# First expert layer: the inner channels of the first product go to the partitions

## The reference, cut to what matters

```
for e in range(8):                                  # experts; each token has its best two
    w_e = sum(where(top_i == e, top_v, 0))
    h = gelu(xf @ fc1_w[e].T + fc1_b[e])            # 192 channels to 512 inner ones
    y = h @ fc2_w[e].T + fc2_b[e]                   # 512 to 192
    out = out + w_e[:, None] * y
shared = gelu(xf @ w1_w.T + w1_b) * (xf @ w3_w.T + w3_b) @ w2_w.T + w2_b
```

## Time and profile before

| | |
|---|---|
| median of 3 runs | 450.82 us (450.76 to 451.69) |
| the profiled execution: its own time | 451.97 us |
| its span | 450.0 us |
| PE busy | 405.9 us, 90% of the span |
| DVE, ACT, POOL busy | 58%, 41%, 29% |
| share of PE in the chain that ended last | 79% |
| layer 0's blocks, first product of block 0 to y of block 22 | 56.45 to 149.0 us |

### The profile page before, as it was taken

The page is one execution under the profiler, slowest core; times in us unless marked ns, Lnnn a source line. Parts: engine busy times, 40 slices in busy tenths (PEclk is TensorE's granted clock), DMA queues, the critical chain, the costliest instruction groups (busy, mean ns, idle before and its releaser), DMA issues.

```text
span 450.0 us, 7988 instructions
## 1 busy us (share of the span) xinstructions
PE 405.9 (90%) x2303; PEld 299.8 (67%) x2304; DVE 262.5 (58%) x673; ACT 186.5 (41%) x463; POOL 128.4 (29%) x137
## 2 busy tenths in 40 slices
PE   0999998999999899988888877999989999999995
PEld 0755365666667888866766655744667877778884
DVE  4535514222222187789898974574676767677744
ACT  1024232122222115798787863333344444444410
POOL 4301124455554100000000000002255555555530
PEclk9999999999999999999999999999999999999999
DMA  8999201111110387000000087780011111110006
GB/s 224 258 305 330 52 17 36 39 45 46 33 33 9 102 263 328 1 1 1 1 2 1 1 213 208 180 230 13 16 46 34 33 37 36 44 49 23 0 0 210
DMA packets 20888, 39.41 MB, mean 88 GB/s; under 512 B 5711, under 2 KB 14965, under 8 KB 20418
## 3 DMA queue, kind: packets, MB, share of 16 engines
q1 hardware_dynamic: 11362, 29.66, 22.9%
q0 software_dynamic: 5280, 6.85, 5.3%
q10 hardware_dynamic: 4224, 2.62, 2.1%
HBM read 36.21 MB, written 7.93 MB: 98 GB/s over the span
## 4 chain that ended last, share of the span: by engine, by line
PE 79%; ACT 6%; DMA 6%; DVE 4%; issue 3%; POOL 0%; ACTq 0%; DVEq 0%; SPq 0%; POOLq 0%
PE bank L1368 14%; PE bank L1282 12%; PE bank L1344 9%; PE bank L1349 8%; PE bank L1537 5%; PE bank L1360 4%; PE bank L1491 4%; DMA w_first<-y_rows 3%; PE bank L1553 3%; PE bank L1326 2%; PE bank L1355 2%; PE bank L1354 2%; PE bank L1268 2%; PE bank L1585 2%; ACT scratch L755 2%
## 5 line engine op out<-in xcount | busy, mean ns | idle before, releaser
L549 POOL DMA_INDIRECT rows<-xn_rows,slot_tok x56 | 59.4, 1061 | 89.1 <-DVE slot_tok L935 51.6
L557 POOL DMA_INDIRECT y_rows<-y,slot_row x54 | 56.0, 1036 | 86.5 <-DVE y L1003 46.1
L1368 PE MATMUL bank<-w_second,hid_t 128*128 x370 | 70.9, 331 | 6.5 <-issue 3.6
L1368 PEld LDWEIGHTS bank<-w_second,hid_t 128*128 128x128 f32 x370 | 58.7, 190 | 10.6 <-issue 10.5
L1349 PE MATMUL bank<-w_first,rows_t 128*128 x124 | 45.3, 488 | 0.4 <-issue 0.4
L1005 DVE TENSOR_TENSOR y<-bank,w_second 128x192 f32<-128x192 f32 x23 | 8.2, 358 | 63.6 <-PE bank L1368 63.6
L1344 PE MATMUL bank<-w_first,rows_t 96*128 (+1 forms) x92 | 43.5, 595 | 1.1 <-issue 1.0
L988 DVE COPY hid_t<-bank 128x384 f32<-128x384 f32 (+1 forms) x54 | 33.0, 612 | 19.2 <-PE bank L1360 13.8
L654 ACT ACTIVATE act_h<-bank 128x512 f32<-128x512 f32 x23 | 13.7, 597 | 69.6 <-PE bank L1344 69.6
L597 POOL COPY act_h<-o_inv 128x256 f32<-128x256 f32 x12 | 4.8, 402 | 122.7 <-DVE o_inv L1169 122.7
L659 ACT ACTIVATE act_g<-bank 128x384 f32<-128x384 f32 x31 | 15.2, 492 | 51.4 <-PE bank L1355 51.4
(11 more groups left out here) (198 smaller groups left out, 790.8 us busy)
## 6 DMA issues: line engine op xcount, KB each, us to landing
w_first<-in_gate_up SPq DMA_DIRECT2D x16, 384.0 KB, 6.5
w_second<-in_down SPq DMA_DIRECT2D x1, 4608.0 KB, 17.4
w_first<-in_fc SPq DMA_DIRECT2D x1, 3072.0 KB
w_second<-in_fc SPq DMA_DIRECT2D x1, 3072.0 KB, 28.2
w_first<-in_gate_up_rest SPq DMA_DIRECT2D x16, 192.0 KB, 7.2
rows<-xn_rows,slot_tok POOLq DMA_INDIRECT x56, 2.7
y_rows<-y,slot_row POOLq DMA_INDIRECT x54, 2.3
w_first<-in_x_t SPq DMA_DIRECT2D x2, 384.0 KB, 4.5
```

Source lines behind the costliest of these rows:

```text
L549: pool.indirect_dma_start(rows[b % 2][:, 0:ROW[L.l]], None, xn_rows[L.l], bass.IndirectOffsetOnAxis(slot_tok[:, b:b + 1].bitcast(U32), 0), ...
L557: pool.indirect_dma_start(y_rows[L.l], bass.IndirectOffsetOnAxis(slot_row[:, b:b + 1].bitcast(U32), 0), y[b % 2][:], None, bounds_check=TO ...
L1368: ins = pe.matmul(bank[:, 1, 0:C], hid_t[:, tile(ic)], w(P, ic * C, C), start=(ic == 0), stop=(ic == L.IC - 1))
```

## The change

In layer 0 the operands of the first product change places. For each of 4 pieces of 128 inner channels and each of 2 halves of the channels, the array holds a 96 (or 97) x 128 piece of the weights, and `rows_t`, 128 columns, is streamed: bank 5 gets the inner channels in partitions and the 128 rows along the free dimension, in 4 pieces. Gelu's output is what the second product holds, so the 4 transposes and the copy to `hid_t` are gone. `act_h` and `hid_t` become the two buffers of Gelu's output. The weights come from `first_w`, two buffers of 97 x 1024 in `scratch`, to which DVE copies the block's weights in two instructions (`copy_weights`), some blocks ahead; DVE does the `value_load` of row 0 and PE doesn't any more. The first product of b now waits for the copies and for Gelu of b-1 (it reads bank 5). DVE's loop body is: copies for b, result of b-2.

```diff
+        self.first_w_ready = sem(f"L{n}_first_w_ready")
...
+        hid_b = [act_h, hid_t]
+        first_w = [scratch_at(2048 + u * NCH * I0, NCH, I0) for u in range(2)]
...
+        def act_block0(act, L, b, u):
+            act.wait_ge(L.first_ps, b + 1)
+            nc.scalar.activation(hid_b[u][:], bank[:, 5, :], ACT.Gelu).then_inc(L.hid_ready, 1)
...
+            def copy_weights(L, b, u):
+                at = dve.value_load(blk_weights[0:1, 0, bass.ds(b, 1)], min_val=0, max_val=(L.E - 1) * L.sizes[0])
+                if not isinstance(b, int) or b >= 2:
+                    dve.wait_ge(L.first_ps, b - 1)
+                for k in range(NCH):
+                    w = w_first[0:CH + k, k * I0:(L.E - 1) * L.sizes[0] + (k + 1) * I0][:, bass.ds(at, I0)]
+                    v.tensor_copy(first_w[u][0:CH + k, k, :], w).then_inc(L.first_w_ready, 1)
...
             def blocks(L):
+                dve.wait_ge(s_fc1, 32)
+                dve.wait_ge(L.expert_ready, len(L.sizes))
+                copy_weights(L, 0, 0)
+                copy_weights(L, 1, 1)
                 dve.wait_ge(s_fc2b, 16)
-                dve.wait_ge(L.expert_ready, len(L.sizes))
-                hid_copy(L, 0)
+                copy_weights(L, 2, 0)
                 result(L, 0, 0, 0)
-                hid_copy(L, 1)
+                copy_weights(L, 3, 1)
                 result(L, 1, 1, 0)
                 w_low_parts()
-                with dve.Fori(0, (L.NB - 3) // 2) as i:
+                with dve.Fori(0, (L.NB - 5) // 2) as i:
                     for u in range(2):
-                        b = i * 2 + (u + 3)
-                        hid_copy(L, b - 1)
-                        result(L, b - 1, u, i + 1)
-                hid_copy(L, L.NB - 1)
-                result(L, L.NB - 1, (L.NB - 1) % 2, (L.NB - 1) // 2)
+                        b = i * 2 + (u + 4)
+                        copy_weights(L, b, u)
+                        result(L, b - 2, u, i + 1)
+                copy_weights(L, L.NB - 1, (L.NB - 1) % 2)
+                for b in (L.NB - 3, L.NB - 2, L.NB - 1):
+                    result(L, b, b % 2, b // 2)
...
             def first(L, b, w, u):
                 pe.wait_ge(L.rows_t_ready, b + 1)
                 if L.l == 0:
-                    for k in range(NCH):
-                        kr = CH + k
-                        ins = pe.matmul(bank[:, 5, :], rows_t[0:kr, k, :], w(kr, k * I0, I0),
-                                        start=(k == 0), stop=(k == NCH - 1))
+                    pe.wait_ge(L.first_w_ready, NCH * (b + 1))
+                    if not isinstance(b, int) or b > 0:
+                        pe.wait_ge(L.hid_ready, b)
+                    for ic in range(L.IC):
+                        for k in range(NCH):
+                            kr = CH + k
+                            ins = pe.matmul(bank[:, 5, tile(ic)], first_w[u][0:kr, k, tile(ic)], rows_t[0:kr, k, :],
+                                            start=(k == 0), stop=(k == NCH - 1))
                     ins.then_inc(L.first_ps, 1)
...
             def hid_transpose(L, b):
+                if L.l == 0:
+                    return
...
-                pe.wait_ge(L.hid_t_ready, b + 1)
+                hid = hid_t if L.l else hid_b[u]
+                pe.wait_ge(L.hid_t_ready if L.l else L.hid_ready, b + 1)
...
-                    w1 = weights(L, i * 2 + 3, 0)
+                    w1 = first_weights(L, i * 2 + 3)
```

More of the change, by code:

```diff
@@ L649, in act_rows @@
                            ).then_inc(L.rows_t_ready, 1)
+        def act_block0(act, L, b, u):
+            act.wait_ge(L.first_ps, b + 1)
+            nc.scalar.activation(hid_b[u][:], bank[:, 5, :], ACT.Gelu).then_inc(L.hid_ready, 1)
         def act_block(act, L, b):
             act.wait_ge(L.first_ps, b + 1)
[L653 to L659, removed]
+            if not isinstance(b, int) or b > 0:
+                act.wait_ge(L.hid_ready, b)
+            nc.scalar.activation(act_g[:], bank[:, 5, 0:I1], ACT.Silu).then_inc(L.gate_act, 1)
         def rest_of(start):
@@ L694, in act_blocks @@
         def act_blocks(act, L):
-            act_block(act, L, 0)
+            act_block0(act, L, 0, 0)
             act_rows(act, L, 1)
@@ L701, in act_blocks @@
                     b = i * 2 + (u + 1)
-                    act_block(act, L, b)
+                    act_block0(act, L, b, 1 - u)
                     act_rows(act, L, b + 1)
@@ L1336, in weights, with first_weights @@
                 return part
+            def first_weights(L, b):
+                return weights(L, b, 0) if L.l else None
             def first(L, b, w, u):
@@ L1361, in hid_transpose, with second @@
                 ins.then_inc(L.hid_t_ps, 1)
-            def second(L, b, w, first_block=False):
-                pe.wait_ge(L.hid_t_ready, b + 1)
+            def second(L, b, w, u, first_block=False):
+                hid = hid_t if L.l else hid_b[u]
+                pe.wait_ge(L.hid_t_ready if L.l else L.hid_ready, b + 1)
                 if not first_block:
@@ L1367, in second @@
                 for ic in range(L.IC):
-                    ins = pe.matmul(bank[:, 1, 0:C], hid_t[:, tile(ic)],
+                    ins = pe.matmul(bank[:, 1, 0:C], hid[:, tile(ic)],
                                     w(P, ic * C, C),
@@ L1374, in blocks @@
                 pe.wait_ge(L.expert_ready, len(L.sizes))
-                w0 = weights(L, 0, 0)
+                w0 = first_weights(L, 0)
                 pe.wait_ge(L.sh_g_ready, 2 * L.IC)
@@ L1386, in blocks @@
                 hid_transpose(L, 0)
-                first(L, 1, weights(L, 1, 0), 1)
+                first(L, 1, first_weights(L, 1), 1)
                 rows_transpose(L, 2, 0, 1)
-                second(L, 0, weights(L, 0, 1), True)
+                second(L, 0, weights(L, 0, 1), 0, True)
                 hid_transpose(L, 1)
-                first(L, 2, weights(L, 2, 0), 0)
+                first(L, 2, first_weights(L, 2), 0)
                 rows_transpose(L, 3, 1, 1)
-                second(L, 1, weights(L, 1, 1))
+                second(L, 1, weights(L, 1, 1), 1)
                 with pe.Fori(0, (L.NB - 3) // 2) as i:
-                    w1 = weights(L, i * 2 + 3, 0)
+                    w1 = first_weights(L, i * 2 + 3)
                     for u in range(2):
@@ L1403, in blocks @@
                         if u == 0:
-                            w1 = weights(L, b + 1, 0)
-                        second(L, b - 1, w2)
+                            w1 = first_weights(L, b + 1)
+                        second(L, b - 1, w2, u)
                 hid_transpose(L, L.NB - 1)
-                second(L, L.NB - 1, weights(L, L.NB - 1, 1))
+                second(L, L.NB - 1, weights(L, L.NB - 1, 1), (L.NB - 1) % 2)
             pe.wait_ge(s_const, 16)
```

## The result

Over 20 runs each the changed kernel takes 449.73 us (median), the kernel before 451.98; the ratio is 0.9924 with an interval of 0.99 to 0.9948. The ratio leaves out the slowest runs, more than 1.5% above the fastest of their kernel (two of the changed kernel's, one of the other's). In the profiled executions the span went from 450.0 to 447.3 us. The forecast range of 438.0 to 446.5 does not hold the median.

The account below looks back on a forecast made before the run. PE was taken to bound the blocks, GpSimd's loop close behind. Start 1.8, 14 middle blocks 3.5, 4 last blocks 1.1 and end 1.4 gave 7.8 us: 450.82 to 443.0, range 438.0 to 446.5.

Parts of the forecast that it names:

- The start: Layer 0's first blocks: despite two copies delaying block 0, block 4 begins at 70.7 in place of 72.50, 1.8 us earlier.
- The starting point: Time of the kernel before, from which the gain was subtracted: 450.82 us, the median of the runs shown.
- The loop through GpSimd takes over: Blocks 4 to 18: second product, y, scatter, gather, landing pace them; 3.70 us a block for 3.95, 3.5 us won.
- the hold of the copies on a scatter: DVE's weight copies against GpSimd's DMAs: 0 to 0.73 us a loop possible, 0.08 taken.
- the 1.06 row: Profile row: a GpSimd DMA beside DVE's multiplications from SBUF took 1.06 us, losing 0.04; basis for the copies' cost.
- second rival: Blocks: copies hold up every second loop's scatter, 0.21 us a block, 3.87; gain 4.6, 446.2 us; chance 0.19.
- The last four blocks: Blocks 18 to 22: GpSimd's loop is 0.5 us shorter; 3.42 us a block for 3.70, 1.1 us won.
- the end: Block 22's first product to its second: 3.31 us in place of 4.71, 1.4 us won.
- What bounded the kernel before: Layer 0's blocks: PE paces them, 3.68 us of work a block plus some 0.2 of number loads in its sequencer.
- The first product: PE, each block: 16 pairs of weight load and 128-column matmul at 0.111 us, 1.79 in all, 0.07 more than before.
- Rival 4: First product: weight loads of 0.19 us don't hide, blocks of 4.56 us; slower, 459.6 us; chance 0.04.
- rival 3: Blocks: copies hold up both scatter and gather, 0.73 us a block; slower, 455.5 us; chance 0.06.

Follow-up runs that it names:

- 1: Changed kernel with four idle products of 256 columns filling PE's pause before block 0's first product: 447.46 us, ratio 0.9864.
- 2, e2_early: Changed kernel with DVE's weight copies for blocks 0 and 1 moved ahead of the shared expert's last tile: 445.54 us, ratio 0.9829.
- 3, e10_before_pause: Kernel before, with three useless DVE copies lengthening PE's pause before block 0 to about 2.0 us: 455.79 us, ratio 1.0076.
- 5: Changed kernel with the early copies for blocks 0 and 1, and DVE copying 16 columns, not 512, from block 4 on: 443.05 us, ratio 0.9804.
- 4, e3_late: Changed kernel with copies for block b started only after the first product of b-1, not b-2: 451.34 us, ratio 0.9922.
- 7: Kernel before, with gather(b + 4) ahead of scatter(b) in GpSimd's queue in layer 0: 448.43 us, ratio 0.9908.
- 8: Changed kernel with both the early copies for blocks 0 and 1 and layer 0's gathers ahead of scatters: 437.55 us, ratio 0.9656.
- e4_gather: Changed kernel with gather(b + 4) ahead of scatter(b) in GpSimd's queue in layer 0: 444.51 us, ratio 0.9814.

## Why the prediction was wrong, and where it was right

**The start: the step that failed most.** I had block 4 at 70.7, and it came at 73.67. The copies took the time that I gave them (block 0 at 57.47 for 57.2, block 1 at 60.67 for 60.4), but I put them down as 0.75 us of delay and nothing else: the sum has no term for the clock, and the only clock that I had read was the 1.00 of blocks 4 to 22. The pause of PE grew from 0.99 to 2.03 us, and the clock went to its lower level for 6.8 us behind it. Shown from both sides: filled or removed, the pause leaves the clock up and block 4 at 70.88 and 69.80 (1, 2); made in the kernel before, it brings the fall and some 3 us (3). The start is 3.0 of the 5.1 us missing between the two profiles (2.7 for 7.8), and the fall is 2.8 of these 3.0 (73.67 for 70.88). The changed kernel's own 20 runs say the same: the four with a mean clock of 1.0 took 445.4 to 446.8 us, inside or next to the forecast range; the ten at 0.992, with a fall of this length somewhere, 447.8 to 451.4. So the pause seems to be followed by the fall in most runs and not in all; a mean clock does not say where in a run it fell.

**The starting point.** The median missed by more than 5.1 us, 449.73 for 443.0. I had taken the time from the 450.82 of three runs; over 20 runs the kernel before has 451.98, so 1.2 of the 6.7 us lie there and not in the change.

**The loop through GpSimd takes over: right, but its price came out near by luck.** It gave 3.75 us a block where I had 3.70 and PE idled before the row transposes as described. The loop itself is 3.58, not 3.66 (5), and the copies add 0.17 in the changed kernel (0.21 in e2_early), where I had 0.04: the one term was too long by 0.08 and the other too short by 0.13, and the two nearly cancel. The mis-sized term is the hold of the copies on a scatter: 0.43 us in every second block, not 0.08 a loop. I leaned on the 1.06 row because its neighbour had one tensor operand, but that neighbour was a multiplication that took 0.2 us for 128 columns; the copies take 0.34 for 512 (a pair 0.76, one 0.42), less than half as long a column, at the short end of the 0.35 to 0.69 that I gave them. The Trainium skill (SBUF — State Buffer, "SBUF: two separate sides") speaks of just this kind of copy: whichever of the two takes the shared ports first keeps the other out. Here the trace agrees that each can hold up the other (scatters of 1.45, copies of 0.97 in 4), but which of them began first does not decide it: copies that began 0.15 us into a scatter left it at 1.04, copies that began 0.5 into it made it 1.39. My second rival, the time by that rule, had the hold almost right, 0.21 a block; its 3.87 was too high because it too stood on a loop of 3.66.

**The last four blocks and the end.** 0.6 for 1.1, the copies' hold again (three of the four scatters there took 1.41 to 1.46); my 3.42 had also left out the 0.04 of the copies, and with it the term is 1.0. At the end 0.5 for 1.4: I let the last two second products follow in a stream, and forgot that bank 1 is single; y stands between them, 2.2 us from start to start, not 1.3.

**What bounded the kernel before: half right.** PE's work of 3.68 a block was right to the hundredth (7), but the 0.27 on top I gave to the number loads. It was the gathers' landing, with a number load queued behind it. This did not hurt the sum, as both causes were to go or to turn into the loop's 3.66, but it hid that the old kernel could be freed of 0.27 us a block by an edit of two lines.

**The first product: right.** 16 pairs at 0.111 us, 1.78 in all, and 3.317 us a block once nothing else stands in the way (8). Rival 4 has fallen, and so has rival 3: from block 4 on every gather but the first (1.18) took 1.03 us. With the gathers ahead of the scatters in both kernels, and the copies early, the change is worth 10.9 us: from 448.43 us (7) to 437.55 (8), on the same chip.

## What to carry to other kernels

When an edit puts work in front of a stage, ask not only how late the stage starts but how long TensorE stands idle there: here one microsecond of copies cost three more through the clock, and the copies fitted into an idle time of the same engine a little earlier. When the pacing engine is relieved, look for the loop that runs just behind it and price it from its own rows; here a queue order (a gather behind a scatter that waits for the result) took most of the gain, and turning the order round gave it back. Fast copies of VectorE within SBUF that overlap GpSimd's DMAs belong in the sum of that loop.

## What the runs showed of the hardware that I had not expected

A pause of TensorE of 2.0 us before the blocks, not one of 1.0, was followed by 6.8 us at 1.2 GHz in all four profiles that have it (the changed kernel, e3_late, e4_gather and e10_before_pause) and, going by the mean clocks, in most of their other runs; none of the seven profiles with the pause of 1.0 us has such a fall there. The fall came 1.6 to 1.7 us after work had resumed with 128-column products, and 1.4 us after it with 512-column ones (3). A scatter of GpSimd took 1.45 to 1.47 us when a pair of DVE's fp32 copies within SBUF (0.76 us) had begun 0.2 us before it, 1.02 to 1.08 when they began up to 0.2 us behind its start, 1.39 to 1.44 when they began 0.51 to 0.56 us behind it, and 1.02 with copies of 16 columns. Copies that had begun 0.09, 0.23, 0.32 and 0.41 us before it made it 1.56, 1.42, 1.33 and 1.24 long in e4_gather: such a scatter ended 1.65 us behind the copies' start each time. When they began 0.61 or 0.62 us behind it, the scatter took 1.02 and the copies 0.97. Copies moved by 0.4 us cost the same as before (4): where both hang on one loop, a shift does not separate them.
